# A fused block on one core: moved scatters, a router inside the first expert tile, and an earlier gate half

## The chip, the cores and the metric

One Trainium2 chip, one of its cores. The engines are TensorE (matmul), VectorE, ScalarE, GpSimd and SyncE; each runs its own instruction list in order, and they meet at semaphores. The metric is the device time of one launch in microseconds (us), the median of the runs shown.

## The reference

The input x is 4 batches of 512 tokens of 256 features, float32. The block does, for each batch:

```
h  = layernorm(x) * (1 + ca) + sa                 # modulation from a small matrix product of c
q, k, v, g = h @ wq + bq, h @ wk + bk, h @ wv + bv, h @ wg + bg      # 16 heads of 16
ret = ((q k^T) * decay mask) v                    # retention, per head
ro  = group norm of ret over all tokens and the head's 16 features, scaled and shifted
x   = x + ga * ((silu(g) * ro) @ wo + bo)
h2  = layernorm(x) * (1 + cb) + sb
logits = h2 @ gate_kernel                         # 8 experts, the best 2 per token, softmax of the two
x   = x + gb * sum over the two experts e of weight_e * ((silu(h2 @ w0_e) * (h2 @ w1_e)) @ wo_e)
```

An expert has 512 hidden features. 2048 tokens with 2 experts each are 4096 rows to push through experts.

## The kernel before, in words

There are two stages that overlap. The **front** loops over the 4 batches (b = 0 to 3). In round b the engines do the projections and the retention of batch b, and, in between, the late steps of earlier batches: group norm, output product, second norm and modulation of batch b - 1, and router, top 2 and row numbers of batch b - 2. The order is written out by hand for each engine. The **expert stage** takes the routed rows in 39 tiles of 128 rows.

*From tokens to rows.* For each batch VectorE takes the logits (`take_logits`, L1098), picks the best two (`choose_top`, `choose_places`), computes their weights (`choose_weights`, which needs a tanh by ScalarE, `top_tanh`), and, from a running count per expert that TensorE sums up (`rank`, L1559), the row number of each token in its expert's region of the DRAM buffer `routed` (`places`, `rows_of_tokens`). GpSimd then scatters the batch's modulated rows with eight indirect DMAs (`scatter`, L560, four groups of 128 tokens, two experts each). A row also carries the token number, the weights and the output gate gb; `gb_copies` on ScalarE fills in the last.

*Tables.* Which expert a tile belongs to and where its rows begin is computed on the chip, twice. The first table, made when batches 0 and 1 are counted, serves the first `EARLY` = 8 tiles, which hold rows of these two batches only; they run while batches 2 and 3 are still being finished. The second table (`tiles_of_experts(1)` to `table_rows(1)`) serves tiles 8 to 38. ScalarE fills up each expert's region with pad rows (`pads`, nine DMAs of 260.5 KB from L850 and L745). SyncE loads the rows of a tile (`load_rows`, L435); before tile 8 it waits for the second table, for the pads and for all scatters (L450 to L453).

*A tile* (`pe_step` and its counterparts `act_step`, `dve_step`): its 128 rows are loaded to `rowbuf`; TensorE transposes them (`turn_rows`, L1605); VectorE copies the transposed rows (`take_rows`, which also copies the rows' metadata once `added_ok` allows it); TensorE multiplies by w0 and w1 of the expert (the two halves of `upward`: L1688 for the first 8 tiles, L1697 to L1701 later); ScalarE does a tanh, VectorE two products (`silu_mul`, `hidden`); TensorE transposes the result (`turn_hidden`, L1709), ScalarE copies it (`turn_back`), TensorE multiplies by wo (`down`, L1717), VectorE scales it (`weighted`, L1315), and GpSimd adds it to the output in DRAM with an indirect DMA that accumulates (`add_rows`, L602). Step i of TensorE also does the transposes of tile i + 1 and the down projection of tile i - 1. `add_rows(i)` waits until addition i - 1 has landed, then raises `added_ok` by one, then waits for the result of tile i. `take_rows(i)` needs `added_ok` at i + 1; it starts at 4.

*Where the stages meet.* After the last round of the front, each engine has a hand-written list for the last part of batch 3, the router of batch 2 and tiles 0 to 7: L1344 to L1381 on VectorE, L1753 to L1776 on TensorE, L798 to L854 on ScalarE, L591 to L635 on GpSimd. The group norm of batch 3 goes: VectorE's statistics, TensorE's average over a head (`average`, L1518), VectorE's deviation and its square (`group_center`, L1058), a second average (`average_dev`, L1525), a power on GpSimd (`group_power`), scale and shift on VectorE (`group_scale`), the normalisation on ScalarE (`group_normed`), the product with the gate (`gated`), the output product (`out_rows`, L1530). On GpSimd the second norm's power of batch 3 (`second_scale`) stands between the halves of batch 2's scatter.

*Banks.* PSUM banks 6 and 7 serve the late steps in turn. `tail_items` (L67) lists these steps in the order in which they take a bank, and a step waits until the step two places ahead has been drained (for the last batch's own h2 transposes, logits and rank: one place). Four other banks serve the front; a group of scores waits until the step four places ahead is drained, which for the last group of the first four is gate half 1. A gate half (`gate`, L681) is emptied by ScalarE in two instructions, an identity and a tanh.

Of the kernel before, what the change touches and what calls it, by code (L numbers as in the profile page):

```python
# [66 lines left out]
def tail_items():  # L67

    items = []
    for b in range(B + 1):  # L70
        if 2 <= b < B:
            items.append((b - 2, "logits", "dve"))
        if 2 <= b < B:
            items.append((b - 2, "rank", "dve"))
        if b == B - 1:
            items.append((b, "counts", "dve"))
        if b == B:
            items.append((b - 2, "logits", "dve"))
        if b >= 1:
            items.append((b - 1, "gn", "dve"))  # L80
        if b == B:
            items.append((b - 2, "rank", "dve"))
        if b == B - 1:
            items.append((b, "firsts", "dve"))
        if b < B:
            items += [(b, "stE", "dve"), (b, "stO", "dve")]
        if b >= 1:
            items += [(b - 1, n, "dve") for n in ("wo01", "wo23")]
        if b == B - 1:
            items.append((b, "fold", "dve"))  # L90
        if b >= 1:
            items += [(b - 1, "h2T0", "act"), (b - 1, "h2T1", "act")]
    return items + [(B - 1, "logits", "dve"), (B - 1, "rank", "dve")]
# [33 lines left out]
def adaln_block(nc, x, wq, bq, wk, bk, wv, bv, wg, bg, wo, bo, gn_w, gn_b, gamma,  # L127
                gate_k, w0, w1, wo_e, c, wmod, out):
    ctx = ExitStack()
    with ctx:  # L130
# [336 lines left out]
        def _(pool):  # L467
# [92 lines left out]
            def scatter(b, tiles):  # L560

                if 0 in tiles:
                    settle(pool, [(idx_ready, b + 1), (row_ready, b + 1), (gb_copied, b + 1),
                                  (h2_ready, b + 1)], pool_passed)
                for t in tiles:
                    for k in range(TOPK):
                        g.indirect_dma_start(routed, bass.IndirectOffsetOnAxis(ap=idx[:, k, t:t + 1], axis=0),  # L567
                                             h2[b][:, t, :], None).then_inc(scattered, 16)
# [52 lines left out]
            for i in range(EARLY):  # L621
                add_rows(i, i, first=i == 0)
                if i == 0:
                    modulate(B - 1)
                if i in (2, 3):
                    scatter(B - 1, (2 * i - 4, 2 * i - 3))
                if i == EARLY - 4:
                    pool.wait_ge(tab_ready, 4)
            pool.wait_ge(x2_last, 16)
# [9 lines left out]
        def _(act):  # L639
# [8 lines left out]
            def normed(b):  # L648

                act.wait_ge(shift1, b + 1)  # L650
                if b:
                    act.wait_ge(tail.full, tail.filled(b - 1, "stO"))
                for t in range(NC):
                    i = NC * b + t
                    a.activation(xn[:, t, :], tile_of_x(i), ACT.Identity, scale=rs1[:, i:i + 1],
                                 bias=nmr1[:, i:i + 1]).then_inc(xn_ready, 1)
# [24 lines left out]
            def gate(b, ft):  # L681

                act.wait_ge(front.full, front.filled(b, f"g{ft}"))
                a.activation(z[:, ft, :], front.bank(b, f"g{ft}")[:, :], ACT.Identity,
                             bias=bg_s[:, ft:ft + 1]).then_inc(z_ready, 1)
                a.activation(th[:, ft, :], front.bank(b, f"g{ft}")[:, :], ACT.Tanh, scale=0.5,
                             bias=bgh_s[:, ft:ft + 1]).then_inc(z_ready, 1)
                act.wait_ge(z_ready, 2 * (FT * b + ft + 1))
                act.sem_inc(front.drained["act"], 1)
# [57 lines left out]
            def top_tanh(b):  # L747
                act.wait_ge(vd_ready, b + 1)
                a.activation(vt[:, :], vd[:, :], ACT.Tanh, scale=0.5).then_inc(vt_ready, 1)
# [7 lines left out]
            for b in range(B):  # L757
                p, final = b - 1, b == B - 1
                queries(b, 0)
                if b == B - 1:  # L760
                    act.wait_ge(gb_out, 16)
                if b:
                    load_expert(2 * b)
                if p >= 1:
                    top_tanh(p - 1)
                queries(b, 1)
                if b == 0:
                    a.mul(bgh_s[:, :], bg_s, 0.5).then_inc(bgh_ready, 1)
                    act.wait_ge(bgh_ready, 1)
                keys(b, 0)  # L770
                if b:
                    load_expert(2 * b + 1)
                keys(b, 1)
                if b == 0:
                    load_expert(0)
                    load_expert(1)
                if p >= 1:
                    gb_copies(p - 1)
                if p >= 0:
                    group_normed(p)  # L780
                    act.wait_ge(prod_ready, FT * p + FT)
                gate(b, 0)
                if not final:
                    normed(b + 1)
                    gate(b, 1)
                if p >= 0:
                    second_normed(p)
                if final:
                    first_rows()
                if not final:  # L790
                    features(b + 1)
                if p >= 0:
                    store_x(p)
                if p >= 0:
                    if p == 0:
                        act.wait_ge(mod2_ready, 2)
                    h2_features(p)
            b = B - 1  # L798
            gate(b, 1)
            top_tanh(b - 1)  # L800
            group_normed(b)
            gb_copies(b - 1)
            act.sem_inc(it_act, 1)

            def turn_back(i, s):
# [31 lines left out]


            act_step(0, 0)
            act_step(1, 1)  # L840
            second_normed(b)
            h2_features(b, [0])
# [15 lines left out]
        def _(dve):  # L858
# [170 lines left out]
            def gates(b, ft):  # L1029

                dve.wait_ge(z_ready, 2 * (FT * b + ft + 1))
                v.scalar_tensor_tensor(out=z[:, ft, :], in0=th[:, ft, :], scalar=1.0, in1=z[:, ft, :],
                                       op0=ALU.add, op1=ALU.mult).then_inc(z_done, 1)
# [311 lines left out]
            group_center(b)  # L1345
            take_rows(0, 0)
            gates(b, 1)
            take_logits(b - 1)
            choose_top(b - 1)
            group_variance(b)  # L1350
            group_scale(b)
            choose_places(b - 1)
            choose_weights(b - 1)
            take_rows(1, 1)
            gated(b)
            silu_mul(0, 0)
            hidden(0, 0)
            places(b - 1)
            rows_of_tokens(b - 1)
# [26 lines left out]
        def _(pe):  # L1386
# [366 lines left out]
            b = B - 1  # L1753
            pe.sem_inc(it_full, 2)
            pe.sem_inc(dn_full, 2)
            project(b, "g", wg_s, 1)
            average(b)
            turn_rows(0, 0)
            router(b - 1)
            average_dev(b)  # L1760
            pe.wait_ge(we_in, 16 * 3 * E)
            pe_step(0, 0, before_down=lambda: rank(b - 1))
            out_rows(b)

            def banks_drained():
# [36 lines left out]
```

## Time and profile before

| | |
|---|---|
| median of 3 runs | 408.25 us (405.19, 408.25, 408.51) |
| the profiled execution | 404.72 us, of which the span is 403.0 |
| mean granted TensorE clock in the span | 0.964 of full speed |
| busy: TensorE, VectorE, GpSimd, ScalarE | 365.5 (91%), 260.8 (65%), 231.6 (57%), 173.5 us (43%) |
| chain that ended last, by engine | TensorE 67%, VectorE 10%, DMA 7%, issue 5%, GpSimd 5%, ScalarE 3% |
| DMA | 49.05 MB, mean 122 GB/s |

In the profile, PE is TensorE, PEld its weight loads, DVE VectorE, ACT ScalarE, POOL GpSimd, SP SyncE; a q behind the name is the engine's sequencer, which issues DMAs and waits. L12 is line 12 of the kernel. Times count from the start of the span. The front runs to about 157 us; tile 0 begins at 160; tiles 8 to 38 fill the rest. The busy shares are averages over both stages, so the text goes by the stretches around the changed steps.

### The profile page before, as it was taken

Reading aid. Unit: us, or ns where it says so; the run is one execution under the profiler, and the core shown is the slowest. Engines: PE = TensorE matmul, PEld = TensorE weight load, DVE = VectorE, ACT = ScalarE, POOL = GpSimd, SP = SyncE. Lnnn points to the kernel's source line nnn. Section 1 sums busy time; section 2 is a strip of 40 time slices with the busy share of each in tenths; the row PEclk is TensorE's granted clock in tenths of the full one; section 3 lists DMA queues with packets and bytes.
Section 4 is the critical chain, followed back from the end, with each engine's and each line's share of the span. In section 5 each row is a group of like instructions: output and inputs, shape, how many; then the busy total and the mean of one; then the engine's idle time right before and its main releaser. Section 6 shows DMA issues by size and latency. Waiting matters only on the chain.

```text
span 403.0 us, 11501 instructions
## 1 busy us (share of the span) xinstructions
PE 365.5 (91%) x3893; PEld 272.0 (67%) x3894; DVE 260.8 (65%) x728; ACT 173.5 (43%) x264; POOL 231.6 (57%) x173
## 2 busy tenths in 40 slices
PE   3897799899999888999995999999999999999980
PEld 3464557766775676656553788888888888888860
DVE  5557627846855785847753677777777777777740
ACT  3334246453463313343122265555555555555520
POOL 3112520663691746177475277777777777777751
PEclk9999899999999997799997899999999999999995
DMA  6955081066447324254596333333344333333222
GB/s 209 315 178 191 3 304 40 25 210 229 162 138 266 148 91 130 72 196 134 125 345 156 66 67 75 67 71 79 79 79 79 79 79 77 69 65 75 44 27 25
DMA packets 32322, 49.05 MB, mean 122 GB/s; under 512 B 3198, under 2 KB 18972, under 8 KB 32284
## 3 DMA queue, kind: packets, MB, share of 16 engines
q1 hardware_dynamic: 11384, 16.98, 15.4%
q0 software_dynamic: 8176, 13.65, 14.9%
q10 hardware_dynamic: 12724, 17.89, 13.2%
q8 instruction: 26, 0.43, 0.4%
q14 instruction: 12, 0.10, 0.1%
HBM read 30.35 MB, written 18.16 MB: 120 GB/s over the span
## 4 chain that ended last, share of the span: by engine, by line
PE 67%; DVE 10%; DMA 7%; issue 5%; POOL 5%; ACT 3%; POOLq 1%; SPq 0%; DVEq 0%; ACTq 0%
PE ps L1717 13%; PE ps L1423 10%; PE ps L1698 7%; PE ps L1697 7%; PE ps L1701 7%; PE ps L1442 4%; PE ps L1709 3%; DMA out_dram<-wg_s,qd 3%; PE ps L1688 3%; DVE sm L1042 3%; POOL routed L567 3%; PE ps L1512 2%; PE ps L1605 2%; PE ps L1537 2%; PE ps L1555 1%
## 5 line engine op out<-in xcount | busy, mean ns | idle before, releaser
L599 POOL TENSOR_TENSOR w_lo<-we,w_hi 128x1024 fp32r<-128x1024 f32 x31 | 77.1, 2488 | 25.8 <-ACT w_hi L825 25.8
L1717 PE MATMUL ps<-we,qeo 128*128 x312 | 76.6, 389 | 1.4 <-ACT qeo L809 0.8
L809 ACT COPY qeo<-ps 128x512 f32<-128x512 f32 x39 | 22.9, 587 | 111.3 <-PE ps L1709 111.3
L1717 PEld LDWEIGHTS ps<-we,qeo 128*128 128x128 f32 x312 | 57.4, 191 | 19.5 <-issue 12.6
L609 POOL DMA_INDIRECT out_dram<-wg_s,qd x30 | 47.0, 1568 | 33.4 <-issue 13.9
L1322 DVE TENSOR_TENSOR w_halves<-we,w_halves 128x1024 fp32r<-128x1024 f32 x31 | 38.0, 1225 | 8.1 <-ACT w_halves L825 8.1
L1294 DVE CAST rT_halves<-ps 128x256 fp32r<-128x256 f32 x31 | 13.2, 424 | 38.9 <-PE ps L1605 38.9
L1688 PE MATMUL ps<-we,xn 128*128 x64 | 34.6, 669 | 0.5 <-issue 0.5
L567 POOL DMA_INDIRECT routed<-h_first,idx x24 | 25.0, 1041 | 15.5 <-DVE idx L1156 8.7
L825 ACT CAST w_hi<-we 128x1024 fp32r x31 | 32.6, 1051 | 0.0
L825 ACT CAST w_halves<-we 128x1024 fp32r x31 | 32.5, 1048 | 0.1
L1697 PE MATMUL ps<-w_halves,rT_halves 128*128 128x512 f32 x62 | 30.2, 487 | 0.0
L1302 DVE SCALAR_TENSOR_TENSOR sm<-sm,ps 128x512 f32<-128x512 f32 x39 | 26.4, 678 | 4.8 <-ACT sm L814 4.8
L1309 DVE TENSOR_TENSOR sm<-sm,ps 128x512 f32<-128x512 f32 x39 | 26.5, 681 | 0.8 <-PE ps L1688 0.5
L1697 PE MATMUL ps<-w_hi,rT_halves 128*128 128x512 f32 x62 | 27.0, 435 | 0.0
L1698 PE MATMUL ps<-w_halves,rT_halves 128*128 128x512 f32 x62 | 24.4, 394 | 0.0
L1698 PE MATMUL ps<-w_hi,rT_halves 128*128 128x512 f32 x62 | 24.4, 393 | 0.0
L1709 PE MATMUL ps<-ident,sm 128*128 128x128 f32 x156 | 23.5, 273 | 0.4 <-DVE sm L1309 0.4
L814 ACT ACTIVATE sm<-ps 128x512 f32<-128x512 f32 x39 | 23.6, 604 | 0.0
L1709 PEld LDWEIGHTS ps<-ident,sm 128*128 128x128 f32 x156 | 19.1, 140 | 6.5 <-issue 1.6
L1042 DVE TENSOR_TENSOR sm<-ps,dmask 128x512 f32<-128x512 f32 x32 | 19.8, 680 | 0.7 <-PE ps L1476 0.7
L1423 PE MATMUL ps<-hT,wq_s 128*128 128x512 f32 x32 | 18.5, 715 | 1.9 <-ACT hT L662 1.6
(237 smaller groups left out, 713.9 us busy)
## 6 DMA issues: line engine op xcount, KB each, us to landing
rowbuf<-routed SPq DMA_DIRECT2D x37, 260.5 KB, 2.9
we<-in_ffn_w_kernel_dram ACTq DMA_DIRECT2D x16, 512.0 KB, 4.3
we<-in_ffn_wo_kernel_dram ACTq DMA_DIRECT2D x8, 512.0 KB, 7.0
routed<-z ACTq DMA_DIRECT2D x9, 260.5 KB, 5.3
xs<-in_attn_x_dram SPq DMA_DIRECT2D x4, 512.0 KB, 10.3
out_dram<-xs ACTq DMA_DIRECT2D x4, 512.0 KB, 4.4
we<-in_wmod_dram SPq DMA_DIRECT2D x1, 1024.0 KB, 10.4
sbcb<-gsc_dram SPq DMA_DIRECT2D x4, 256.0 KB, 5.0
```

Source lines behind the costliest of these rows:

```text
L567: g.indirect_dma_start(routed, bass.IndirectOffsetOnAxis(ap=idx[:, k, t:t + 1], axis=0), h2[b][:, t, :], None).then_inc(scattered, 16)
L599: g.tensor_tensor(w_lo[1], expert_up(e, 1), w_hi[1].bitcast(F32), ALU.subtract)\
L609: g.indirect_dma_start(out, bass.IndirectOffsetOnAxis(ap=meta[s % 4][:, TOK - D:TOK - D + 1].bitcast(I32), axis=0), ey[s % 2], None, compu ...
L825: a.copy(w_hi[which], expert_up(e, which)).then_inc(w_hi_ready[which], 1)
L1042: v.tensor_tensor(sm[:, u, j, :, :, :, :].rearrange("p t f q n -> p t (f q n)"), front.bank(b, n)[:, :].rearrange("p (t m) -> p t m", t=2) ...
L1322: v.tensor_tensor(w_lo[0], expert_up(e, 0), w_hi[0].bitcast(F32), ALU.subtract)\
L1423: last = mm(front.bank(b, n)[:, :], s[:, k, ft * P:(ft + 1) * P], hT[:, k, :], start=k == 0, stop=k == FT - 1)
L1688: last = mm(up_ps[s % 2][which][:, :], rT[s % 2][:, k, :], weights(e, (which * FT + k) * F, F), start=k == 0, stop=k == FT - 1)
L1697: mm(dst, rT_hi[s % 2][:, k, :], w_hi[which][:, k * F:(k + 1) * F], start=k == 0, stop=False)
L1698: mm(dst, rT_lo[s % 2][:, k, :], w_hi[which][:, k * F:(k + 1) * F], start=False, stop=False)
L1709: last = tr(ps[5][:, k * P:(k + 1) * P], ein[s % 2][:, k * P:(k + 1) * P], ident[:, :])
L1717: last = mm(down_ps, eit[s % 2][:, k, :], weights(e, 2 * FT * F + k * D, D), start=k == 0, stop=k == KF - 1)
```

## The change

It has three parts.

1. *Where the stages meet.* On TensorE the transposes of tile 0's rows and `average(3)` go ahead of the projection of gate half 1, and the router of batch 2 moves from behind them into step 0, between the first half of the up projection and the transposes of tile 1's rows. In the ring of banks "gn" of batch 3 now stands ahead of "logits" of batch 2. On VectorE variance and scale of the group norm go ahead of the logits of batch 2, and the weights of batch 2 move behind the first product of tile 0. On ScalarE the tanh for batch 2's weights and the copies of gb go behind step 0.
2. *Last scatter.* The scatter of batch 3 is issued behind additions 1 and 2 and no longer behind additions 2 and 3.
3. *Batch 0.* ScalarE empties gate half 1 of batch 0 ahead of the norm of batch 1 (`normed`); the other batches keep the order.

```diff
@@ tail_items
-        if b == B:
-            items.append((b - 2, "logits", "dve"))
         if b >= 1:
             items.append((b - 1, "gn", "dve"))
         if b == B:
-            items.append((b - 2, "rank", "dve"))
+            items += [(b - 2, "logits", "dve"), (b - 2, "rank", "dve")]
@@ gpsimd
                 if i == 0:
                     modulate(B - 1)
-                if i in (2, 3):
-                    scatter(B - 1, (2 * i - 4, 2 * i - 3))
+                if i in (1, 2):
+                    scatter(B - 1, (2 * i - 2, 2 * i - 1))
@@ scalar
                 gate(b, 0)
                 if not final:
+                    if b == 0:
+                        gate(b, 1)
                     normed(b + 1)
-                    gate(b, 1)
+                    if b:
+                        gate(b, 1)
...
             b = B - 1
             gate(b, 1)
-            top_tanh(b - 1)
             group_normed(b)
-            gb_copies(b - 1)
             act.sem_inc(it_act, 1)
...
             act_step(0, 0)
+            top_tanh(b - 1)
+            gb_copies(b - 1)
             act_step(1, 1)
@@ vector
             group_center(b)
             take_rows(0, 0)
             gates(b, 1)
+            group_variance(b)
+            group_scale(b)
             take_logits(b - 1)
             choose_top(b - 1)
-            group_variance(b)
-            group_scale(b)
             choose_places(b - 1)
-            choose_weights(b - 1)
             take_rows(1, 1)
             gated(b)
             silu_mul(0, 0)
+            choose_weights(b - 1)
             hidden(0, 0)
             places(b - 1)
             rows_of_tokens(b - 1)
@@ tensor
+            turn_rows(0, 0)
+            average(b)
             project(b, "g", wg_s, 1)
-            average(b)
-            turn_rows(0, 0)
-            router(b - 1)
             average_dev(b)
             pe.wait_ge(we_in, 16 * 3 * E)
-            pe_step(0, 0, before_down=lambda: rank(b - 1))
+            pe_step(0, 0, between=lambda: router(b - 1), before_down=lambda: rank(b - 1))
             out_rows(b)
```

## Rows read from the trace of the kernel before

**Rows 1.** Groups by line: busy us, mean ns; idle time before them and what ended it.

```profile
L1717 PE MATMUL ps<-we,qeo 128*128 x312 | 76.6, 389 | 1.4 <-ACT qeo L809 0.8 <-DVE wg_s L1315 0.4
```

**Rows 2.** Timeline, TensorE: start, us, line, operation, count; in brackets idle time and releaser.

```profile
218.99 0.69 PE L1605 MATMUL ps<-ident,rowbuf 128*128 128x128 f32 x2 [4.25 <-DMA rowbuf<-routed]
```

**Rows 3.** The chain of waits, 120 to 235: start, us, what.

```profile
175.48 1.04 POOL rs L509
...
210.30 4.44 DMA routed<-h_last,idx
```

**Rows 4.** SyncE's waits, 190 to 222: line and releaser; us in total, times, longest.

```profile
SPq L452 <- DMA routed<-z: 16.2, 1, 16.2
SPq L453 <- DMA routed<-h_last,idx: 0.4, 1, 0.4
```

**Rows 5.** Timeline of batch 0: TensorE and ScalarE around gate half 1.

```profile
33.55 1.98 PE L1423 MATMUL ps<-hT,wg_s 128*128 128x512 f32 x4
37.87 1.20 PE L1476 MATMUL ps<-qeo,kT 32*64 32x128 f32 x64 [2.34 <-ACTq L689]
...
36.44 0.67 ACT L684 ACTIVATE z<-ps,vcol 128x512 f32<-128x512 f32 x1
```

**Rows 6.** Timeline of TensorE where the stages meet.

```profile
154.19 2.75 PE L1423 MATMUL ps<-hT,wg_s 128*128 128x512 f32 x4
...
157.16 1.85 PE L1555 MATMUL ps<-gate_s,kT 128*128 128x8 f32 x16
...
160.31 3.77 PE L1688 MATMUL ps<-we,xn 128*128 x4 [0.53 <-issue]
```

**Rows 7.** Timeline of GpSimd: the modulation of batch 2.

```profile
154.54 2.18 POOL L534 TENSOR_TENSOR h_first<-h_first,sbcb 128x1024 f32<-128x1024 f32 x1 [0.84 <-PE ps L1547]
156.80 2.18 POOL L537 TENSOR_TENSOR h_first<-h_first,sbcb 128x1024 f32<-128x1024 f32 x1
```

**Rows 8.** Timeline of VectorE: group norm of batch 3, routing of batch 2, tiles 0, 1.

```profile
157.28 1.72 DVE L1062 TENSOR_TENSOR gd<-gmv,gav 128x2 f32<-128x2 f32 x1
...
160.25 0.18 DVE L1101 COPY lg<-ps 128x32 f32<-128x32 f32 x1
...
160.95 0.15 DVE L1067 SCALAR_TENSOR_TENSOR gve<-ps,gav 128x2 f32<-128x2 f32 x1
...
162.40 0.08 DVE L1113 MATCH_VALUE_LOAD ix<-mx,lg 128x8 f32 x1
...
164.55 0.42 DVE L1292 COPY xn<-ps 128x256 f32<-128x256 f32 x1
...
167.15 0.69 DVE L1309 TENSOR_TENSOR sm<-sm,ps 128x512 f32<-128x512 f32 x1 [0.17 <-PE ps L1688]
...
169.56 0.17 DVE L1156 CAST idx<-posf 128x8 int32<-128x8 f32 x1
```

**Rows 9.** Busy time by stretch: PE, PEld, DVE, ACT, POOL; granted clock; DMA share; GB/s.

```profile
160.00:161.00 1.00, 0.69 (x1) 0.50 (x2) 0.93 (x8) 0.00 (x0) 0.00 (x0) 0.50 0.53 183
...
166.00:167.00 1.00, 1.00 (x5) 0.50 (x3) 0.98 (x2) 0.00 (x0) 0.00 (x0) 0.92 0.50 127
...
216.00:220.00 4.00, 1.01 (x3) 0.82 (x4) 0.29 (x1) 1.74 (x2) 2.90 (x2) 0.67 0.59 142
220.00:224.00 4.00, 4.00 (x7) 1.93 (x6) 3.59 (x6) 0.00 (x0) 1.04 (x1) 0.50 0.41 98
```

**Rows 10.** Timeline, tiles 5 and 6: VectorE, GpSimd's scatter, ScalarE's second pads.

```profile
194.67 0.17 DVE L1156 CAST idx<-posf 128x8 int32<-128x8 f32 x1
...
197.24 0.29 DVE L1298 COPY qd<-rowbuf 128x265 int32<-128x265 int32 x1
...
203.76 0.48 DVE L1298 COPY qd<-rowbuf 128x265 int32<-128x265 int32 x1 [0.35 <-POOLq L607]
...
199.30 1.00 POOL L567 DMA_INDIRECT routed<-h_last,idx  x1 [0.30 <-issue]
...
203.82 4.92 ACTq L745 DMA_DIRECT2D routed<-z  x4
```

## The prediction, made from the kernel before alone

> **What bounds the kernel now.** I read the groups by line first. The down projection alone keeps TensorE busy for 76.6 us with 1.4 us of idle time before its 312 matmuls [rows 1]; its one large wait there is 4.25 us for a load of routed rows, ahead of tile 8's transposes at 218.99 [rows 2]. From tile 8 on nothing else stops it, so whatever moves tile 8 moves the end by as much. The chain of waits says what sets tile 8: batch 2's row numbers, four scatters on GpSimd, the second norm's power (175.48), batch 3's rows and router, its scatters, the last landing 4.44 us after 210.30, then the load of tile 8's rows [rows 3]. The DMA queue's own waits add what the chain hides: SyncE waits 16.2 us for the pad rows that ScalarE writes, and after them only 0.4 us for the scatters [rows 4]. Two things end within 0.4 us of each other there; advancing the scatters alone buys 0.4 us.
>
> **Sum against one run.** The profiled execution took 404.72 us (span 403.0 and 1.72 around it); the median of the three runs is 408.25, 3.5 above it. I work out a shift and put it on both.
>
> **Third edit, batch 0.** The projection for gate half 1 ends at 33.55 + 1.98 = 35.53, but its emptying starts at 36.44, behind the norm of batch 1, and TensorE sits 2.34 us until 37.87 [rows 5]. Emptied first, it starts at 35.57: 0.87 us earlier. The norm then starts about 2 us later; it is covered by the two score groups and the state products that TensorE does before it transposes, and if that cover went, the 2 us would show. From there to tile 0 the chain is TensorE and VectorE, with no fixed arrival in it. I take -0.9 us; ends 0 (the masks, done by VectorE one after another, absorb it) and -2.3 (the whole wait).
>
> **First edit, group norm.** The average goes ahead of the 2.75 us projection [rows 6], behind the transposes of tile 0's rows. So its result comes near 155.2 and not 157.05. Then VectorE needs two small subtract and square steps. In the trace the first of them took 1.72 us, from 157.28 to 159.00, and GpSimd's modulation of batch 2 ran from 156.80 to 158.98, just after another from 154.54 to 156.72 [rows 7, 8]. Both end together. I read it as a wait for GpSimd: the step started earlier meets the first modulation, the square meets the second, and it ends at 159.2 as before. So the earlier average gains 0; the other end is 2.1 us, if the square gets in between. The Trainium skill, GPSIMD Engine Reference, Key points, says that GpSimd shares its SBUF interfaces with VectorE and contends with Vector instructions with two SBUF inputs, which both steps are. By that rule the gain is the 0 taken; were the long row a coincidence, the sum would be 2.1 us lower, the third rival.
>
> What the projection gains or loses is covered by the same wait: the old router ran in it (157.16 to 159.01 [rows 6]) at no cost. That cover is what the change gives up.
>
> **Router of batch 2.** It now stands between the halves of tile 0's up projection. The first half ran 160.31 to 164.08, twice as long as the later ones, at a granted clock of 0.50, the 1.2 GHz level, from 160 on [rows 6, 9]; TensorE will be idle instead of routing before it, so I keep that level. The router's 1.85 us follow; the clock returned near 166 (0.92 in 166 to 167) [rows 9], so about 1.9 us of it run at half rate and it ends near 166.8. Behind that VectorE has, one after another: logits and top two 160.25 to 160.95, 0.70; places and weights 162.40 to 164.55, 2.15; rows of tile 1, gating and the first product 164.55 to 167.15 less 0.17 of wait, 2.43; the second product, places and row numbers 167.15 to 169.73, 2.58 [rows 8]. That is 7.86; records overlap by some 0.2, so 7.7. Batch 2's row numbers come at 174.5 where they came at 169.73: +4.8. Ends: +2.2 with tile 0 at the full clock (162.19 + 1.85 + 7.9) and +6.0 with the router wholly at half rate. Moving the weights behind the first product, the tanh and the copies of row data behind ScalarE's step 0, and variance and scale ahead of the logits (0.7 us sooner) changes nothing more: each finds its input long there. The swap of two places in the ring of banks costs nothing, since both banks are drained by 155.2. The output product waits for the gating and so for the logits too, some 3 us.
>
> All 4.8 are on the chain: four scatters, the power at 175.48, ScalarE's second norm and the transposes that TensorE already waits for.
>
> **Last scatter.** Eight issues, about 1.21 us each with their gaps on GpSimd (199.30 to 204.15 for four), move from behind additions 2 and 3 to behind 1 and 2. In times of before (all plus the 4.8): batch 3's row numbers come at 194.84, the first four go out from 195.7 to 200.6 instead of 199.30, the other four after addition 2, until 207.7 instead of 211.3 [rows 10]. But additions queue behind them on GpSimd. VectorE may copy tile 5's metadata only when addition 2 has passed its wait for addition 1: 200.6 and not 197.24. Tile 6's comes at 207.7 and not at 203.76, where it already waited 0.35 us for GpSimd. Behind these copies on VectorE stand the gating of tiles 4 and 5 and the final tile table, then done near 212.6. TensorE waits for them twice, about 1 and 2.2 us, and comes to tile 8 some 2.8 us later, at 217.5. The second half of the pads (203.82, 4.92 us to issue) goes 0.7 us later, into a less crowded DMA stretch; I let them land at 213.5 instead of 214.3 (ends 212.7 and 215). So tile 8's rows arrive 1.3 us earlier, at 217.7, and TensorE waits a few tenths and not 4.25 us.
>
> That spares a second thing. After the long wait the granted clock was 0.67 in 216 to 220 and 0.50 in 220 to 224 [rows 9]: work of about 5 us at half rate, 2.5 us lost. With no long wait it stays at 1.00. The scatter part is -1.3 - 2.5 = -3.8; ends 0 (pads at 215, a clock drop after one of the new waits) and -4.5.
>
> **Sum.** -0.9 + 4.8 - 3.8 = +0.1: 404.8 for a run like the profiled one, 408.3 against the median.
>
> **Rivals.**
> - The clock stays at 2.4 GHz in tile 0. For: the dense projection ends some 0.5 us closer to it. Against: nearly 2 us of idle time in between, where the router stood. +2.2 replaces +4.8: -2.5, 405.8.
> - GpSimd queues too much: slower. Place: VectorE's metadata copies of tiles 5 and 6. Price: 3.4 + 3.9 = 7.3 us of delay, of which I let 2.8 reach TensorE. It decides where TensorE comes to tile 8 after its rows, at 217.7: beyond 3 us of delay every microsecond counts, and a new wait of 2.2 us may bring the clock down, as the 4.25 us one did. With 5.7 us reaching TensorE it is +2.8: 411; with all of it 412.6. For: row 203.76 shows that this wait exists. Against: TensorE has 4.25 us to spare.
> - The square gets in between the two modulations. Norm, tile 0 and router come 2.1 us earlier, and closer behind the projection, so at the full clock: 2.2 - 2.1 replaces 4.8, -4.6, 403.6. Against: the gap is 0.08 us [rows 7] and the two steps are tied by a wait.
> - The first two edits do nothing in effect (the logits are no later, as VectorE is late anyway): -0.9 - 3.8, also about 403.6. Against: VectorE took the old logits at 160.25 and has 7.7 us of work behind them.
>
> **Chances.** Forecast 0.45 (406.5 to 410), clock stays 0.18, GpSimd queues 0.22, square or idle edits 0.15. A difference under 1% (4.1 us) can't be told from none here: the three runs of before spread over 3.3 us. Faster by that (under 404.2): nearly all of the last and a part of the second, 0.19. Slower (over 412.3): the far part of the third and an unlucky clock, 0.13. The range 403.5 to 411.8 takes in every case's centre and leaves out the far ends, 2 in 10.
>
> **What would show it.** Right: scores of batch 0 near 37.0; the square still ending with the second modulation; batch 2's row numbers 4 us or so later; waits of VectorE for GpSimd at tiles 5 and 6; TensorE's wait ahead of tile 8 under 1 us at a clock of 1.00 in 216 to 228. Wrong: a square that ends near 157; tile 0's first half in 1.9 us; pads or the table, not the rows, far behind the scatters; a clock drop in tile 6 or 7.

## The result, and the profile after

The changed kernel takes 404.23 us (median of 20 runs, 401.15 to 407.55) against 408.0 (20 runs, 405.19 to 415.39): ratio 0.9916, 95% interval 0.9891 to 0.9941, so some 3.4 us faster. No change (408.3) had been forecast. Medians here and below are of all runs, while each ratio compares the fast runs alone with fast runs of the kernel before from the same series (whose medians were 406.4 to 408.0 us), so a ratio is not the quotient of two medians. The profiled execution took 402.1 us, span 399.8, where that of before took 404.72 and 403.0.

The down projection's group, which answers to [rows 1], is as it was, 75.9 us busy for 76.6:

```profile
L1718 PE MATMUL ps<-we,qeo 128*128 x312 | 75.9, 386 | 1.8 <-ACT qeo L808 0.8
```

TensorE's timeline (start, us, line, operation; in brackets idle time and what ended it). Its lines are one higher than before.

```profile
13.52 5.25 PE L1424 MATMUL ps<-hT,wq_s 128*128 128x512 f32 x8 [0.75 <-ACT hT L660]
18.61 3.60 PE L1424 MATMUL ps<-hT,wk_s 128*128 128x512 f32 x8
...
35.73 1.20 PE L1477 MATMUL ps<-qeo,kT 32*64 32x128 f32 x64 [1.50 <-ACTq L687]
...
153.91 1.96 PE L1424 MATMUL ps<-hT,wg_s 128*128 128x512 f32 x4
...
157.14 1.98 PE L1689 MATMUL ps<-we,xn 128*128 x4 [0.69 <-issue]
158.96 1.85 PE L1556 MATMUL ps<-gate_s,kT 128*128 128x8 f32 x16
...
217.39 0.44 PE L1606 MATMUL ps<-ident,rowbuf 128*128 128x128 f32 x2 [1.41 <-DMA rowbuf<-routed]
217.67 1.88 PE L1689 MATMUL ps<-we,xn 128*128 x4
...
224.19 0.73 PE L1702 MATMUL ps<-w_lo,rT_halves 128*128 128x512 f32 x2
```

Of the kernel before, to go with 217.67:

```profile
219.47 3.62 PE L1688 MATMUL ps<-we,xn 128*128 x4
```

Beside [rows 5] the wait ahead of the scores is 1.50 us and not 2.34. Beside [rows 6] the projection takes 1.96 us, tile 0's first half 1.98 and not 3.77, and the router now follows it. Beside [rows 2] TensorE waits 1.41 us for tile 8's rows and not 4.25, and the half product behind them, the second half of tile 7's up projection, takes 1.88 us and not 3.62.

VectorE's timeline, same columns:

```profile
154.28 1.54 DVE L1063 TENSOR_TENSOR gd<-gmv,gav 128x2 f32<-128x2 f32 x1
155.86 0.16 DVE L1064 TENSOR_TENSOR gd<-gd 128x2 f32<-128x2 f32 x1
...
156.27 1.95 DVE L1299 COPY qd<-rowbuf 128x265 int32<-128x265 int32 x1
...
168.41 0.17 DVE L1157 CAST idx<-posf 128x8 int32<-128x8 f32 x1
...
193.49 0.17 DVE L1157 CAST idx<-posf 128x8 int32<-128x8 f32 x1
...
196.06 0.29 DVE L1299 COPY qd<-rowbuf 128x265 int32<-128x265 int32 x1
...
206.40 0.30 DVE L1299 COPY qd<-rowbuf 128x265 int32<-128x265 int32 x1 [4.17 <-POOLq L605]
```

GpSimd's:

```profile
153.63 2.18 POOL L532 TENSOR_TENSOR h_first<-h_first,sbcb 128x1024 f32<-128x1024 f32 x1 [1.97 <-PE ps L1548]
155.89 2.17 POOL L535 TENSOR_TENSOR h_first<-h_first,sbcb 128x1024 f32<-128x1024 f32 x1
...
194.52 1.00 POOL L565 DMA_INDIRECT routed<-h_last,idx  x1 [2.27 <-DVE idx L1157]
...
198.39 0.97 POOL L565 DMA_INDIRECT routed<-h_last,idx  x1 [0.30 <-issue]
199.67 1.60 POOL L607 DMA_INDIRECT out_dram<-wg_s,qd  x1 [0.30 <-issue]
...
207.22 1.60 POOL L607 DMA_INDIRECT out_dram<-wg_s,wv_s  x1 [0.84 <-DMA out_dram<-wg_s,qd]
```

Read the two side by side, as [rows 7, 8]. The deviation still ends with a modulation (155.82, 155.81), but now with the first one, and the square behind it is through in 0.16 us: it started in the 0.08 us gap between the two. What lasts until the end of the second modulation (158.06; the record ends at 158.22) is now the metadata copy of tile 0, 1.95 us long where most of the later ones take 0.3; nobody needs it soon. Batch 2's row numbers come at 168.41, earlier than the 169.56 of [rows 8] and not 4.8 later; 0.82 us of that stood already ahead of the changed steps. At tile 5 (compare [rows 10]) the metadata copy waits for nothing, though two of the four scatters (the last starts at 198.39) and an addition are still to come; at tile 6 it waits 4.17 us, for the landing of the addition issued at 199.67.

The chain of waits ahead of tile 8 (start, us, what):

```profile
207.32 5.64 DMA routed<-z
...
214.53 2.81 DMA rowbuf<-routed
```

SyncE's waits (line and releaser, total, times, longest) and the stretches that answer to [rows 9]:

```profile
SPq L450 <- DMA routed<-z: 16.1, 1, 16.1
```

```profile
216.00:220.00 4.00, 2.61 (x9) 1.60 (x10) 1.48 (x4) 3.08 (x4) 0.00 (x0) 1.00 0.62 157
220.00:224.00 4.00, 4.00 (x22) 3.26 (x21) 3.05 (x6) 0.78 (x2) 3.82 (x2) 1.00 0.54 99
```

The scatters are gone from the chain and from SyncE's waits [rows 3, 4]; the last pad, landing at 212.96, is what is late next. The granted clock is 1.00 where it was 0.67 and 0.50.

**A scale by stages.** The profiles are of single executions, and these differ by up to 4 us where no edit has acted yet (A of before and of e3). So each is cut at five instructions: A from the start to the first transpose of batch 2's modulated rows; B to its row numbers; C to batch 3's; D to the transposes of tile 8's rows; E to tile 8's first product; F to the end of the span. C is 25.1 to 25.2 everywhere. Some expectations below number the products behind the wait one too high: their "first product of tile 8" is the second half of tile 7, and their "tile 9's first product" is tile 8's, where E ends. All in us, the ratio with its 95% interval; the edits that a kernel has stand in the second column (1 group norm and router, 2 scatter, 3 gate half).

| Kernel | edits | A | B | D | E | F | ratio to before |
|---|---|---|---|---|---|---|---|
| before | none | 152.44 | 17.12 | 24.32 | 6.08 | 177.93 | 1 |
| e1_gate_half | 3 | 153.58 | 16.41 | 24.53 | 5.22 | 178.16 | 0.9994 (0.9952 to 1.0036) |
| e3_router | 1 | 156.24 | 16.89 | 24.56 | 5.01 | 177.99 | 1.0065 (1.0024 to 1.0107) |
| e9_router_again | 1 | 154.41 | 16.77 | 24.21 | 5.23 | 178.69 | 0.9983 (0.9938 to 1.0027) |
| e5_no_scatter | 1, 3 | 153.59 | 16.91 | 25.10 | 4.99 | 178.20 | 0.9984 (0.9949 to 1.0019) |
| e2_scatter | 2 | 152.42 | 16.38 | 23.02 | 3.53 | 179.53 | 0.9926 (0.9881 to 0.9971) |
| e6_no_router | 2, 3 | 154.33 | 16.99 | 23.54 | 3.53 | 178.62 | 0.9936 (0.9905 to 0.9966) |
| e14_no_gate | 1, 2 | 153.98 | 16.89 | 23.42 | 3.53 | 179.19 | 0.9915 (0.9857 to 0.9974) |
| after | all | 151.62 | 16.79 | 23.90 | 3.54 | 178.87 | 0.9916 (0.9891 to 0.9941) |
| e7_after_again | all | 151.09 | 16.91 | 23.79 | 3.53 | 179.48 | 0.9919 (0.9876 to 0.9962) |
| e4_square_late | all, square late | 152.47 | 20.16 | 23.98 | 3.47 | 177.92 | 0.9967 (0.9927 to 1.0007) |
| e13_warm_short | none, wait filled | 152.20 | 15.54 | 23.86 | 3.53 | 178.12 | 0.9969 (0.9924 to 1.0014) |

The ratio column alone says which edit counts: of the kernels that only leave edits out, the five with the scatter edit lie at 0.9915 to 0.9936, the four without it at 0.9983 to 1.0065.

### The profile page after: what moved, and what is told of

Read it like the earlier page. It is cut to its first block, busy times and chain, and to the rows that moved or that the text cites. A ratio compares the mean times of both kernels' runs of the same rounds, so it can differ in the third digit from the quotient of the medians.

```text
span 399.8 us, 11501 instructions
## 1 busy us (share of the span) xinstructions
PE 358.1 (90%) x3893; PEld 267.6 (67%) x3894; DVE 261.8 (65%) x728; ACT 173.4 (43%) x264; POOL 231.5 (58%) x173
## 4 chain that ended last, share of the span: by engine, by line
PE 65%; DVE 15%; DMA 6%; issue 4%; ACT 3%; ACTq 3%; POOL 2%; POOLq 1%; SPq 0%; DVEq 0%
PE ps L1718 13%; PE ps L1424 10%; PE ps L1702 7%; PE ps L1699 7%; PE ps L1698 7%; PE ps L1443 4%; DVE sm L1043 3%; PE ps L1710 3%; PE ps L1513 2%; DMA out_dram<-wg_s,qd 2%; PE ps L1606 2%; PE ps L1538 2%; PE ps L1556 2%; ACTq L742 2%; DMA routed<-z 1%
## 5 line engine op out<-in xcount | busy, mean ns | idle before, releaser
L1718 PE MATMUL ps<-we,qeo 128*128 x312 | 75.9, 386 | 1.8 <-ACT qeo L808 0.8
L1689 PE MATMUL ps<-we,xn 128*128 x64 | 30.2, 594 | 0.7 <-issue 0.7
L1702 PE MATMUL ps<-w_lo,rT_halves 128*128 128x512 f32 x62 | 19.4, 393 | 0.0
```

The lines of the kernel that those rows point to most:

```text
L1689: last = mm(up_ps[s % 2][which][:, :], rT[s % 2][:, k, :], weights(e, (which * FT + k) * F, F), start=k == 0, stop=k == FT - 1)
L1702: last = mm(dst, rT_hi[s % 2][:, k, :], w_lo[which][:, k * F:(k + 1) * F], start=False, stop=k == FT - 1)
L1718: last = mm(down_ps, eit[s % 2][:, k, :], weights(e, 2 * FT * F + k * D, D), start=k == 0, stop=k == KF - 1)
```

## Experiments

### Each edit alone

e1_gate_half is the kernel before with the third edit, e2_scatter with the second, e3_router with the first.

```
e1:  if not final:
+        if b == 0: gate(b, 1)
         normed(b + 1)
-        gate(b, 1)
+        if b: gate(b, 1)
e2: -if i in (2, 3): scatter(B - 1, (2 * i - 4, 2 * i - 3))
    +if i in (1, 2): scatter(B - 1, (2 * i - 2, 2 * i - 1))
e3: -router(b - 1)            # ahead of average_dev(b) and tile 0
    +pe_step(0, 0, between=lambda: router(b - 1), ...)
    ...                       # and the rest of that edit
```

> The kernel before with the third edit alone (gate half 1 of batch 0 emptied ahead of the norm). Theory: the first scores of batch 0 start 0.85 us sooner after the projection of gate half 1 ends (TensorE's wait there 1.5 us and not 2.34), the transposes of batch 1 follow the masks, and the gain of 0.9 to 1.5 us is carried to the end: ratio 0.996 to 0.998. Rival: VectorE's masks absorb it, 0. The stretch from 150 on looks as before.

> The kernel before with the second edit alone (last scatter behind additions 1 and 2). Theory: SyncE is then released by the pads alone, 1 to 2 us earlier than before; VectorE's metadata copy of tile 6 waits some 4 us for GpSimd, TensorE comes to tile 8 about 2 us later, its wait there falls from 4.25 to about 1.5 us and the granted clock stays at 1.00 behind it, so that tile 8's gate and up products begin 3 to 4 us earlier relative to batch 3's row numbers: ratio 0.990 to 0.993. Rival (two releases within 0.4 us of each other, nothing else moves): -0.4 us. Rival (GpSimd queues too much): 1 to 3 us slower.

> The kernel before with the first edit alone (average ahead of the projection, router inside tile 0's step). Theory (the square of the group norm gets in between the two halves of GpSimd's modulation): the square ends about 3 us earlier than before, tile 0's first product starts 2 to 3 us earlier, batch 2's row numbers come 0 to 1 us earlier than before relative to the end of the transposes of batch 2, and the end moves by 0 to -1 us if the clock stays up. Rival (my prediction's step: the square waits for both modulations and the router is added to the path): row numbers 2.2 to 6 us later, ratio 1.005 to 1.012.

Measured: 405.61 us (0.9994), 404.58 (0.9926) and 408.37 (1.0065). The scatter edit alone has the gain of the whole change. The gate half shortens its wait as meant (1.49 us), but the end shows no gain from it that can be told from noise: the interval of e1 holds both 1 and the 0.996 to 0.998 that was expected. e1's TensorE timeline shows one place where time goes:

```profile
43.88 1.16 PE L1419 MATMUL ps<-ident,xn 128*128 128x128 f32 x8 [0.86 <-DVE sm L1045]
46.04 3.68 PE L1426 MATMUL ps<-hT,wq_s 128*128 128x512 f32 x4 [1.00 <-ACT hT L662]
```

The same two in the kernel before:

```profile
44.88 1.94 PE L1416 MATMUL ps<-ident,xn 128*128 128x128 f32 x8
47.68 1.98 PE L1423 MATMUL ps<-hT,wq_s 128*128 128x512 f32 x4 [0.87 <-ACT hT L662]
```

There the transposes ran at half rate and the projection did not; in e1 it is the other way round, and at the projection's end the 1.0 us is gone (49.72 against 49.66). The router edit alone looked slower; in its profile 3.8 us stood already in A, ahead of the first instruction that it moves.

Of e1, which keeps the old order, VectorE's and GpSimd's timeline where the group norm meets the second modulation:

```profile
157.92 0.16 DVE L1066 TENSOR_TENSOR gd<-gd 128x2 f32<-128x2 f32 x1
...
157.95 2.18 POOL L537 TENSOR_TENSOR h_first<-h_first,sbcb 128x1024 f32<-128x1024 f32 x1
```

The square gets through the gap here too, as it does in e2 (156.74, 0.16 us): the projection ahead of the average ran at full rate in these two (1.92 and 1.90 us) and not in the kernel before (2.75). So the gap can be met without the first edit.

### The first edit again

> The first edit alone once more. In its profile before, the 3.8 us that it was behind stood already where batch 2 is turned, ahead of the first instruction that the edit moves. Theory (that was the course of one execution's start; the edit itself is worth nothing): 0.995 to 1.005 of before, and from the turn of batch 2 to batch 2's row numbers 16 to 17.5 us as in every other kernel. Rival (the edit costs 2 to 3 us when it stands alone): 1.004 or more again.

Measured: 405.88 us, 0.9983, B 16.77. The slowdown of e3 did not come back, and B is as in e3. One profile can't explain the median of e3's twelve runs, though, and the two intervals only just overlap (1.0024 to 1.0107, 0.9938 to 1.0027): no gain of the first edit alone is seen, and a loss of a few tenths of a per cent is not excluded.

### The square held back

```
 tl.link(v.tensor_tensor(gd, gmv[:, :, 0], gav[:, :, 0], ALU.subtract))
+tl.link(v.tensor_copy(gve, gb_[:, 0:FT]))   # twice, read by nobody
 v.tensor_tensor(gd2, gd, gd, ALU.mult)
```

> The changed kernel with two small copies from PSUM (0.2 us each, linked) between the deviation and its square in the group norm of batch 3, so that the square comes after GpSimd has begun the second half of the modulation. Theory: the square then waits for the second half, ends about 2 us later than in the changed kernel, and tile 0's first product and batch 2's row numbers come about 2 us later (more if the clock falls): 2 to 4 us slower than the changed kernel, so a ratio to the kernel before of 0.996 to 1.002. Rival (the place of the square doesn't matter): 0.4 us later only.

Measured: 406.6 us, 0.9967, where the changed kernel has 0.9916 to 0.9919. Of e4, VectorE's timeline and TensorE's:

```profile
155.20 1.08 DVE L1063 TENSOR_TENSOR gd<-gmv,gav 128x2 f32<-128x2 f32 x1
156.70 1.83 DVE L1067 TENSOR_TENSOR gd<-gd 128x2 f32<-128x2 f32 x1
```

```profile
159.66 3.60 PE L1692 MATMUL ps<-we,xn 128*128 x4 [0.69 <-issue]
163.04 1.97 PE L1559 MATMUL ps<-gate_s,kT 128*128 128x8 f32 x16
```

The square misses the gap and takes 1.83 us, to the end of the second modulation; tile 0 starts at half rate, and B grows by 3.3 us, far above every other B. Of these, 1.7 us are tile 0's later start (7.19 us behind batch 2's first transpose, 5.52 in the changed kernel) and 1.6 its first half. This is the course that the prediction drew. It costs 3 us at the row numbers in this profile; the 2 us at the end are not clear of noise, since the intervals overlap (0.9927 to 1.0007, and 0.9891 to 0.9941).

### The changed kernel less one edit, and once more

e5_no_scatter puts the scatters back behind additions 2 and 3; e6_no_router leaves out the first edit, e14_no_gate the third; e7_after_again is the changed kernel.

```
e5:  -if i in (1, 2): scatter(B - 1, (2 * i - 2, 2 * i - 1))
     +if i in (2, 3): scatter(B - 1, (2 * i - 4, 2 * i - 3))
e6:  -pe_step(0, 0, between=lambda: router(b - 1), ...)
     +router(b - 1)           # ahead of average_dev(b), and the rest of that edit undone
e14: -if b == 0: gate(b, 1)
      normed(b + 1)
     +gate(b, 1)
```

> The changed kernel with the scatters of batch 3 put back behind the third and fourth additions (the first and third edits alone). Theory (the scatter edit alone carries the gain; the other two cancel): median within 0.4% of before, the load of tile 8 comes again after the wait for the scatters, tile 8's rows are turned some 4.3 us after TensorE could have, and the clock falls to half speed there. Rival (the edits to batch 2's router are worth 1 us or more once the square gets between the modulations): 0.4% to 0.7% faster than before, with batch 2's row numbers at about 168.4.

> The kernel before with the second and third edits (scatter and gate half), the router of batch 2 left ahead of tile 0. Theory (the router edit gives nothing of its own, since the square gets through between the modulations with the router in place when the projection runs at 2.4 GHz): as fast as the changed kernel, ratio to before 0.990 to 0.994, deviation of the group norm at about 156, tile 0's first product at about 158. Rival (the router edit and the gate half are worth something together): ratio 0.996 or more. Rival (the router edit costs what it cost alone, 2.6 us): ratio 0.985 to 0.988.

> The changed kernel once more, beside the others on the same chip. Both theories: 0.989 to 0.994 of before; it gives the scale for the other kernels of this call.

> The first and second edits without the third. Theory (the scatter edit is the whole gain; the edits ahead of it only move where the clock falls): 0.990 to 0.995 of before, as with all three. Rival (the third edit carries a part of it that the router edit would else cost): 0.996 to 1.0.

Measured: 405.71, 403.3, 403.18 and 404.64 us; 0.9984, 0.9936, 0.9919 and 0.9915. Without the scatter edit the gain is gone, and TensorE waits 5.03 us for tile 8's rows again, as expected; without either of the others the gain stays. In e6 the router still stands ahead of tile 0 and B is 16.99. Its deviation came at 159.93, not near 156, and tile 0's first product at 162.21, not near 158, since the projection took 3.49 us: my expectation for these rows failed. In the old order B is 15.5 to 16.4 us where the square got through the gap (e1, e2, e13) and 17.0 to 17.1 where the deviation waited for the second modulation (before, e6). In the new order the square got through in every profile but e4's, and B is 16.8 to 16.9. So the two orders cost about the same, and the old one varies more with the clock.

### The clock behind the wait at tile 8

The kernel before, with products read by nobody ahead of TensorE's wait for tile 8's rows:

```
 def turn_rows(i, s):
+    if isinstance(i, int) and i == EARLY:
+        for _ in range(16):    # 8 in e13_warm_short
+            mm(ps[7][:, 0:D], ident, hT[:, 0, 0:D], start=True, stop=True)
```

> The kernel before with 16 products more (128 x 256, their result read by nobody) ahead of TensorE's wait for tile 8's rows, which fill that wait. Theory (2.5 us of the scatter part were the clock that falls in the wait): the first product of tile 8 takes 1.88 us instead of 3.2, and the run is 1.3 to 2.5 us faster than before (0.994 to 0.997). Rival (the wait itself and not the clock after it is what the scatter edit took away): 0.998 to 1.002.

Measured: 406.71 us, 1.0000 (0.9963 to 1.0037). It decided nothing about the end: the 16 products (the profile counts each as two) took twice what I had meant and outlasted the wait (D 26.81, E 3.47).

```profile
217.57 7.07 PE L1603 MATMUL ps<-hT,ident 128*128 128x256 f32 x32
```

> The kernel before with 8 products more (128 x 256, read by nobody) ahead of TensorE's wait for tile 8's rows: 3.5 us by the 7.07 us that 16 of them took, inside the wait of 4.25 us. Theory (2.5 us of the scatter part were the clock that falls in the wait): tile 8's rows are turned when they land, some 24.3 us after batch 3's row numbers as before, its first product takes 1.88 us instead of 3.62, tile 9's first product comes 1.5 to 2.5 us earlier than the 30.4 us after batch 3's row numbers of the kernel before, and the run is 0.994 to 0.997 of before. Rival (the clock gained is given back within the next tiles): the first product is shorter, the run 0.998 to 1.002.

Measured: 404.21 us, 0.9969 (0.9924 to 1.0014). TensorE's timeline of e13:

```profile
212.80 3.62 PE L1603 MATMUL ps<-hT,ident 128*128 128x256 f32 x16
216.75 0.44 PE L1608 MATMUL ps<-ident,rowbuf 128*128 128x128 f32 x2 [0.33 <-DMA rowbuf<-routed]
217.02 1.88 PE L1691 MATMUL ps<-we,xn 128*128 x4
...
220.28 0.58 PE L1700 MATMUL ps<-w_halves,rT_halves 128*128 128x512 f32 x1
```

With the scatters as late as ever and the wait filled, E is 3.53 us, as in the kernels with the scatter edit (3.47 to 3.54). So the 1.5 to 2.5 us by which E is longer without the edit are the clock that falls in the wait; the profiles of e10 and e13 show this. That filling the wait makes the whole run faster is not shown: the interval holds 1.

### What is late next

Two edits to the changed kernel: tiles 2 and 3 keep their metadata in buffers of their own, so that those of tiles 6 and 7 need no addition, and SyncE issues half of the pads behind its load of tile 6.

```
+meta_own = two blocks of dmask        # for tiles 2 and 3
-dve.wait_ge(added_ok, i + 1)
+if not (isinstance(i, int) and i in (6, 7)): dve.wait_ge(added_ok, i + 1)
 SyncE: load_rows(6, 6)
+       pads(range(E // 2, E))         # no longer on ScalarE
```

> The changed kernel with two edits at what now stands ahead of tile 8: tiles 2 and 3 keep their metadata in buffers of their own, so that the metadata copies of tiles 6 and 7 wait for no addition, and the pads of experts 4 to 7 are issued from SyncE's queue behind the load of tile 6 instead of from ScalarE's. Theory (tile 8 is held by the landing of the third addition, through tile 6's metadata copy and the table, and by the last pad): the copy of tile 6 comes at about 202.2 instead of 206.40, the table is written at about 207, the last pad lands by about 208, the load of tile 8 comes at 208 to 209.5 instead of 214.53 and the run is 3 to 6 us faster than the changed kernel. Rival (the DMA engines are the limit, pads, scatters and additions sharing them): the pads land at 212 to 213 all the same and the gain is under 1 us. Rival (TensorE's own work of tiles 5 to 7 fills the time): the load comes early but tile 8's rows are turned less than 2 us earlier.

Measured: 402.38 us, 0.9894 (0.9841 to 0.9946), A 155.44, D 22.23. VectorE's timeline, SyncE's waits, TensorE's wait and the DMA share (last column but one) of e8:

```profile
206.09 0.49 DVE L1309 COPY qd<-rowbuf 128x265 int32<-128x265 int32 x1
...
211.35 0.48 DVE L1326 SCALAR_TENSOR_TENSOR wg_s<-ps,qd 128x256 f32<-128x256 f32 x1 [1.10 <-POOLq L615]
211.94 0.18 DVE L1234 TENSOR_SCALAR tabi<-ps 1x31 int32<-1x31 f32 x1
```

```profile
SPq L460 <- DMA routed<-z: 6.4, 1, 6.4
SPq L461 <- DMA routed<-h_last,idx: 3.1, 1, 3.1
```

TensorE's transposes of tile 8's rows:

```profile
219.66 0.44 PE L1616 MATMUL ps<-ident,rowbuf 128*128 128x128 f32 x2 [1.45 <-DMA rowbuf<-routed]
```

The DMA share:

```profile
204.00:210.00 6.00, 5.96 (x24) 3.38 (x23) 3.26 (x13) 1.08 (x2) 4.78 (x5) 1.00 1.03 313
210.00:216.00 6.00, 5.81 (x24) 3.35 (x23) 2.99 (x9) 1.08 (x2) 1.91 (x2) 1.00 0.93 290
```

Counted from the start of the instruction that writes batch 3's row numbers (197.43, 193.49 in the changed kernel), tile 6's metadata comes after 8.66 us where the changed kernel has 12.91, as expected, and the table after 14.51 (17.28). But tile 8's rows are turned only 1.6 us sooner, where the load was to come 5 to 6.5 and the run 3 to 6 us sooner. After the pads SyncE waits 3.1 us for the scatters again, with the DMA engines full from 204 to 216, as they are in the changed kernel from 200 to 212 (1.07 and 1.02). That speaks for the rival of shared DMA engines, and is not a proof of it. TensorE's own work is not what holds tile 8: it still waits 1.45 us for the rows. It is the fastest version run, but its interval and that of the changed kernel overlap.

### TensorE kept busy at the start

e11_warm_start is the changed kernel, e12_all is the kernel of e8, each with 13 products (128 x 128, read by nobody) in TensorE's waits before 13.5 us.

```
 last.then_inc(setup_pe, 1)
+keep_busy(8)    # 2 more behind the modulation's columns, 3 ahead of the first projection
```

> The changed kernel with 13 products more (128 x 128, read by nobody) in TensorE's waits between 4.5 and 13.5 us. Theory (executions differ by up to 5 us where batch 2 is turned because the first projections run at half rate for 5.3 to 10 us of the trace, as the start falls out): the first group of eight products takes about 3.8 to 4.5 us instead of 5.25 to 6.6, batch 2 is turned at 150 to 152, and the run is 1 to 3 us faster than the changed kernel (0.984 to 0.989 of before). Rival (the columns of the modulation come later by what was added and nothing is won): 0.991 to 0.996.

> The kernel with own metadata buffers and with half of the pads on SyncE's queue, with the same 13 products at the start. Theory: the gains add, 0.980 to 0.986 of before, with tile 8's rows turned at 213 to 216. Rival (nothing won at the start): 0.988 to 0.993, as without the products.

Measured: 408.58 us (1.0096, 1.0047 to 1.0144) and 408.83 (1.0045, 1.0005 to 1.0086). Both expectations failed. Beside the kernels that they start from, the products cost about 1.8% (1.0096 to 0.9916) and 1.5% (1.0045 to 0.9894). TensorE's timeline of e11, and one stretch:

```profile
14.02 3.68 PE L1431 MATMUL ps<-hT,wq_s 128*128 128x512 f32 x8
...
44.59 3.78 PE L1431 MATMUL ps<-hT,wq_s 128*128 128x512 f32 x4 [0.87 <-ACT hT L660]
```

```profile
40.00:50.00 10.00, 7.46 (x143) 4.35 (x142) 3.36 (x12) 3.15 (x5) 6.33 (x6) 0.66 0.04 9
```

The first eight products run at full rate, as meant, and the transposes of batch 1 start 1.06 us sooner (41.78). Then the granted clock is 0.66 in 40 to 50 and 0.83 to 0.87 in 100 to 110, 120 to 130, 140 to 150 and 160 to 170 (the changed kernel, up to 170, is below 0.9 only in 150 to 160, at 0.84), and A is 162.53 us, 11 longer. This execution was the slowest of e11's twelve (412.05 us), so it overstates the loss. By these shares the clock takes at most some 8 of the 11 us. Why it falls more often from there on, and where the rest goes, stays open.

## Why the prediction was wrong

The time lay inside its range, but the forecast was no change and the kernel became faster. By its steps:

**Third edit, -0.9.** The wait shrank by 0.84 us, as worked out. Whether it reaches the end is not shown: e1 is at 0.9994 and leaving the edit out changes nothing (0.9915), but 0.9 us are 0.2% and both intervals are wider. The step "from there to tile 0 the chain is TensorE and VectorE" left out that the clock of the groups on that chain can change with when they come, as it did in e1's profile. Over all profiles without the extra products at the start, A is 153.16 us in the mean of the seven with the edit (e8 with 155.44 among them) and 153.89 of the seven without (e10 with 155.57 among them), and each seven spread over 4 us: neither 0 nor 0.9 is excluded.

**Group norm, 0.** The step "the square meets the second" modulation failed. It got through the gap between the two, the third rival's course. The edit is not needed for that (e1, e2): the row of before that the step was read from came late, behind a projection of 2.75 us that ran partly at half rate. The Trainium skill, GPSIMD Engine Reference, Specifications, names VectorE's instructions with two SBUF inputs and those in a two-port mode as the ones that contend with GpSimd. The deviation (two inputs, 1.54 us) agrees, and so does e4's square (1.83). The square in the gap (0.16) shows that the rule decides nothing without the moment at which the instruction comes, and the copy with one input took 1.95 us as well; whether it ran in a two-port mode no run here shows.

**Router of batch 2, +4.8.** This is the step that made the forecast wrong: batch 2's row numbers came 0.3 us sooner (B 16.79, before 17.12) and not 4.8 later. It kept tile 0 where it was, behind the square's wait, and at the 1.2 GHz level; in the changed kernel tile 0 started sooner and ran at full rate (1.98 us). Counted from batch 2's first transpose (152.44, 151.62), the router was to end after 14.4 us and ended after 9.2 (160.81). Of these 5.2 us, tile 0's earlier start is 2.35, its first half 1.95 and the router at full rate 0.87. What VectorE does behind the router was right: 7.8 us, forecast 7.7. In e4, where the square waits and tile 0 is at half rate again, the cost is 3.0 us beside before's B and 3.3 beside the changed kernel's, so the size was too large even there. The rival that said so came to 403.6 and had a chance of 0.15 shared with idle edits; the measured median is 404.23.

**Last scatter, -3.8.** Right in its kind. The rows come earlier by 0.4 us in the two profiles and 0.9 in the mean of the five kernels of the table without the edit and without extra products against the six with it, e4 among them (24.54 to 23.61), where 1.3 was forecast; the last pad, forecast 18.7 us behind batch 3's row numbers, landed 19.3 behind them (212.96). The clock's share is 2.54 us between the two profiles (6.08 to 3.54), forecast 2.5. That it fits so well is luck: the forecast was read from this one profile of before, and in the same means the share is 1.8. Not forecast: 0.75 us given back in F (178.19 to 178.94 in the same means). In the changed kernel one place of it is seen: from tile 9's transposes to tile 10's it takes 5.88 us (222.93 to 228.81), in the kernel before 5.16. GpSimd is late there with tile 8's weight remainder (221.18 to 224.14), behind an addition (220.18). In e2 the profile names that remainder as what TensorE's product waited for:

```profile
224.16 0.73 PE L1701 MATMUL ps<-w_lo,rT_halves 128*128 128x512 f32 x2 [0.30 <-POOL w_lo L599]
```


Of the delays on GpSimd, tile 5's failed: VectorE was to wait for GpSimd's scatters, 5.8 us behind batch 3's row numbers (200.6 against 194.84), and went on 2.4 us behind them (196.06 against 193.66). GpSimd had passed its own wait and raised the semaphore while its scatters were still queued, to run until 199.4. Tile 6's came out at the forecast time, 12.7 us behind the row numbers for 12.9, but by luck: what it waited for was the landing of an addition and not GpSimd's queue. TensorE had the time to spare for it, as said.

**What stays open.** By the stage means the scatter edit is worth 0.9 + 1.8 - 0.75, some 2 us; by the medians about 3.4. C does not differ, nor does B apart from e4. The means of A over the same kernels do, by 1.4 us (154.05 and 152.65), or 0.9 with e10 and e13 on one side and e8 on the other (154.00 and 153.05), but no run here shows how an edit that first acts at 194 us could do that. One profile of each kernel is too little to split it.

## What to carry to other kernels

When a wait ends for two reasons a few tenths apart, count also what the engine loses after the wait: here, by the stage means, the slower clock was worth twice as much as the earlier rows (1.8 and 0.9 us). Time won far upstream of such a point can be lost on the way, as in e1's profile; measure an upstream edit alone, and not by one profile. Cut the profiles to be compared at the same instructions, and repeat a single edit that surprises before explaining it. When a step is read from one row of a profile, look at what clock that row's stretch ran at.

## What the runs showed of the hardware that was not expected

- Three VectorE instructions of 0.16 to 0.3 us otherwise (a subtract and a square of 128x2, a copy from SBUF to SBUF) that started while a 2.18 us GpSimd operation ran lasted until its end (1.54, 1.83, 1.95 us), yet the square that started in a gap of 0.08 us between two such operations took 0.16 us. A copy from PSUM that started in the second of them (155.94 in the changed kernel) took its usual 0.42 us.
- GpSimd raises a semaphore ahead of indirect DMAs that stand before it in the program: tile 5's copy ran at 196.06 with the scatters going until 199.4.
- 13 products of no use in the first 13.5 us cost about 1.8% beside the changed kernel (e11, 1.0096 to 0.9916), though they made the first group of projections 1.57 us shorter (5.25 to 3.68).
- The first eight products of the changed kernel took 5.25 us, against 3.60 for the next eight, while the column of the granted clock reads 1.00 in 14 to 20 us. The trace holds no clock record there before 16.71 us, and the column counts a stretch without one as full: at the start the instructions' durations tell more.
